# Kept partial sums added by VectorE, two small operations of a step on GpSimd, and a rearranged end, in a two-layer graph network kernel

## The reference, cut to what matters

```python
def _ggc(x, adj, W, wih, whh, bih, bhh):
    m = adj @ (x @ W)
    gi = m @ wih.T + bih
    gh = x @ whh.T + bhh
    r = sigmoid(i_r + h_r)
    z = sigmoid(i_z + h_z)
    n = tanh(i_n + r * h_n)
    return (1.0 - z) * n + z * x
h = relu(_ggc(x, adj, W1, ...)); g = relu(_ggc(h, adj, W2, ...))
x1 = layernorm(x + g)
support = x1 @ weight
mask = (adj != 0)
rank = cumsum(mask, axis=1)
deg = rank[:, -1:]
k = minimum(deg, 100)
pos = rank - (deg - k)
w = mask * where(pos > 0, 0.5 ** (k - pos), 0.0)
out = layernorm(x1 + w @ support + bias)
```

## Time and profile before

| | |
|---|---|
| median of 3 runs | 347.71 us (347.25 to 347.92) |
| profiled execution | 348.46 us, span 346.7 us |
| TensorE busy | 329.2 us, 95% of the span |
| VectorE busy | 302.2 us, 87% |
| ScalarE busy | 185.4 us, 53% |
| GpSimd busy | 27.5 us, 8% |
| DMA | 107.86 MB, mean 311 GB/s |
| granted TensorE clock | full, but for the last slice |

### The profile page before, as it was taken

The page is one execution under the profiler, slowest core; times in us unless marked ns, Lnnn a source line. Parts: engine busy times, 40 slices in busy tenths (PEclk is TensorE's granted clock), DMA queues, the critical chain, the costliest instruction groups (busy, mean ns, idle before and its releaser), DMA issues.

```text
span 346.7 us, 6773 instructions
## 1 busy us (share of the span) xinstructions
PE 329.2 (95%) x2540; PEld 154.3 (45%) x2540; DVE 302.2 (87%) x505; ACT 185.4 (53%) x243; POOL 27.5 (8%) x35
## 2 busy tenths in 40 slices
PE   1998999999999999999999999999999999999992
PEld 0442334333333333333333333545444444789992
DVE  0689879898999999997999678879989999978995
ACT  0203304105122057069458347888797969769983
POOL 2000000000000000000000001000210202013264
PEclk9999999999999999999999999999999999999997
DMA  7999999999999999999998999998999996000002
GB/s 244 414 411 408 409 408 400 384 411 393 372 372 375 366 396 358 328 346 353 317 321 288 384 401 391 353 340 325 366 373 349 364 366 215 11 7 4 2 32 93
DMA packets 32001, 107.86 MB, mean 311 GB/s; under 512 B 3553, under 2 KB 6369, under 8 KB 31969
## 3 DMA queue, kind: packets, MB, share of 16 engines
q1 hardware_dynamic: 31104, 106.15, 81.4%
q10 hardware_dynamic: 864, 1.28, 1.0%
HBM read 106.37 MB, written 1.05 MB: 310 GB/s over the span
## 4 chain that ended last, share of the span: by engine, by line
PE 70%; DMA 10%; ACT 8%; DVE 7%; issue 3%; POOLq 0%; POOL 0%; ACTq 0%; DVEq 0%; SPq 0%
PE m_acc L494 35%; PE out L494 15%; DMA stream<-in_adj_t 9%; PE out L626 6%; PE m_acc L626 4%; PE gate_ps L570 4%; PE gate_ps L577 2%; ACT wexp L806 2%; ACT codes L806 2%; DMA w<-in_w 2%; DVE run L1034 1%; PE gate_ps L599 1%; DVE codes L1179 1%; PE gate_ps L594 1%; ACT mx L766 1%
## 5 line engine op out<-in xcount | busy, mean ns | idle before, releaser
L494 PE MATMUL m_acc<-stream,s_in 128*64 128x512 f32 x488 | 119.2, 596 | 1.3 <-DMA stream<-in_adj_t 1.0
L990 DVE TENSOR_SCALAR codes<-stream 128x1024 uint8<-128x1024 f32 x109 | 72.0, 686 | 6.3 <-DMA stream<-in_adj_t 6.0
L494 PE MATMUL out<-stream,s_mid 128*64 128x512 f32 x264 | 66.3, 593 | 0.0
L494 PEld LDWEIGHTS m_acc<-stream,s_in 128*64 128x64 f32 x488 | 32.9, 137 | 63.6 <-issue 49.2
L494 PE MATMUL m_acc<-stream,s_mid 128*64 128x512 f32 x224 | 51.6, 599 | 0.0
L925 POOL TENSOR_TENSOR rstd<-stat,mhalf 128x4 f32<-128x4 f32 x16 | 24.6, 1535 | 311.7 <-DVE stat L1145 311.7
L1039 DVE SCALAR_TENSOR_TENSOR codes<-codes,run 128x384 uint32<-128x384 uint32 (+2 forms) x62 | 43.9, 709 | 2.1
L1034 DVE TENSOR_TENSOR run<-run,codes 128x768 uint16<-128x768 uint16 (+2 forms) x61 | 42.3, 694 | 2.0
L709 ACT ACTIVATE m_high<-m_acc 64x512 f32<-64x512 f32 x13 | 7.7, 594 | 56.1 <-PE m_acc L494 47.2
L494 PEld LDWEIGHTS out<-stream,s_mid 128*64 128x64 f32 x264 | 18.9, 137 | 37.0 <-issue 36.3
L743 ACT ACTIVATE rz<-gate_ps,b_rz 128x256 f32<-128x256 f32 x32 | 13.4, 468 | 36.8 <-PE gate_ps L577 36.8
(11 more groups left out here) (171 smaller groups left out, 402.3 us busy)
## 6 DMA issues: line engine op xcount, KB each, us to landing
stream<-in_adj_t SPq DMA_DIRECT2D x192, 512.0 KB, 6.1
wexp<-in_adj_t SPq DMA_DIRECT2D x2, 512.0 KB, 5.6
late<-in_adj_t SPq DMA_DIRECT2D x2, 512.0 KB, 6.5
third<-in_x_pairs SPq DMA_DIRECT2D x8, 128.0 KB, 6.3
out_nodes<-stream SPq DMA_DIRECT2D x8, 128.0 KB, 2.0
hx<-in_x_pairs ACTq DMA_DIRECT2D x1, 512.0 KB, 7.5
third<-in_adj_t SPq DMA_DIRECT2D x1, 512.0 KB, 7.8
run<-in_adj_t SPq DMA_DIRECT2D x1, 512.0 KB, 9.7
```

Of the source, the lines that this page charges most:

```text
L494: last = nc.tensor.matmul(to[D * u:D * (u + 1), :], state[:, t * D:(t + 1) * D], data[:, u * CW:(u + 1) * CW], start=start[u], stop=stop)
L990: nc.vector.tensor_scalar(edges(p // 2, b, 2 * (p % 2), 2), loaded(n), 0.0, None, ALU.not_equal).then_inc(mask_made, 1)
```

## The change

Chunks 11 to 15 (`WITH_KEPT`): ScalarE's `high` and TensorE's identity products are gone. VectorE's new `high_kept` adds the upper half of the accumulator and the kept sum into `m_high`, behind the first group of chain tiles of the step, and `combine` follows it. In steps 1 to 7 GpSimd does `split_low` and `add_bias`, in this order, behind its power. Step 1 has its chain tiles cut otherwise and ScalarE's expansions all behind its square; step 3 has one expansion more ahead of `split_high` and one fewer behind it. Which engine expands which of the later blocks is dealt anew (21 by VectorE instead of 22). The weights of block (4, 1) lie in `hx` instead of `kept`. In the end other chunks are scaled by ScalarE, and the last chunk's blocks 5 to 7 run in two halves of its nodes, each with its own bank, adds, square, sum, power, scaling and store.

```diff
+WITH_KEPT = range(NCH + 3, 2 * NCH)
+BY_POOL = 7
+PLACE[4, 1] = "h"
 BY_DVE = [AHEAD[4], AHEAD[6], AHEAD[7], AHEAD[8]] + \
-    [REST[n] for n in (2, 5, 7, 9, 11, 12, 14, 16, 18, 19, 21, 22, 24, 26, 28, 30, 32, 34)]
+    [REST[n] for n in (2, 5, 7, 9, 11)] + \
+    [(6, 5), (7, 3), (7, 4), (7, 5), (0, 6), (3, 6), (5, 6), (6, 6), (7, 6), (1, 7), (2, 7), (5, 7)]
-ACT_EXPANDS = {1: (1, 1, 1), 2: (1, 2, 2), 3: (1, 2, 3), 4: (1, 2, 2), 5: (1, 2, 2),
+ACT_EXPANDS = {1: (0, 2, 1), 2: (1, 2, 2), 3: (1, 3, 2), 4: (1, 2, 2), 5: (1, 2, 2),
-ACT_END = (1, 1, 1, 1, 1, 0, 0, 0)
-DVE_END = (2, 2, 1, 1, 1, 1, 0, 0)
+ACT_END = (1, 1, 2, 1, 1, 0, 0, 0)
+DVE_END = (1, 1, 3, 1, 1, 0, 0)
+DVE_SCALES = {5: (0,), 6: (1, 2)}
-OUT_ACT = (0, 2, 4)
+OUT_ACT = (3, 4, 5)
+LAST = NCH - 1
+SPLIT_FROM = 5
+HALVES = (slice(0, KT // 2), slice(KT // 2, KT))
-CHAIN_CUT = [(1, 2), (2, 4), (2, 3), (2, 3)] + [(1, 2)] * 3 + [(0, 1)] * 2
+CHAIN_CUT = [(1, 2), (1, 3), (2, 3), (2, 3)] + [(1, 2)] * 3 + [(0, 1)] * 2
...
-                if first and ch in KEPT:
-                    half, _, part = kept_part(ch)
-                    pe.wait_ge(m2_kept, len(KEPT))
-                    for u in range(2):
-                        nodes = slice(u * HW, (u + 1) * HW)
-                        nc.tensor.matmul(acc_bank(g)[u * D:(u + 1) * D, nodes], ident2[half, :],
-                                         part[:, nodes], start=False, stop=False)
...
+            def share_last():
+
+                for part, tiles in enumerate(HALVES):
+                    for j in range(SPLIT_FROM, NCH):
+                        if part == 0:
+                            if (j, LAST) in BY_DVE:
+                                pe.wait_ge(by_dve, BY_DVE.index((j, LAST)) + 1)
+                            else:
+                                pe.wait_ge(by_act, BY_ACT.index((j, LAST)) + 1)
+                        last = share_tiles(j, LAST, range(tiles.start, tiles.stop))
+                    last.then_inc(last_done, 1)
...
                 if t < NCH:
-                    high(g + 1)
+                    if g + 1 not in WITH_KEPT:
+                        high(g + 1)
                     state(g + 1)
...
+            def add_bias(s):
+                pool.wait_ge(x1_made, s + 1)
+                pool.wait_ge(bias_centred, 3)
...
+                nc.gpsimd.tensor_tensor(x1b_nodes(s), x1, bias_b[:, :, :], ALU.add)\
+                    .then_inc(x1b_made, 1)
+
+            def split_low(s):
+                pool.wait_ge(sup_high, s + 1)
+                nc.gpsimd.tensor_tensor(support(s)[:, :, 1, :], sup_f, support(s)[:, :, 0, :],
+                                        ALU.subtract).then_inc(sup_made, 1)
 
             for s in range(NCH):
                 to_rstd(s, 0)
+                if s < BY_POOL:
+                    split_low(s)
+                    add_bias(s)
...
+            def high_kept(g):
+                _, _, part = kept_part(2 * NCH - 1 - g)
+                dve.wait_ge(pair_used, USED[g])
+                dve.wait_ge(m2_kept, len(KEPT))
+                dve.wait_ge(m_ready, g)
+                nc.vector.tensor_tensor(m_high[0:D, :], acc_bank(g)[D:P, :], part, ALU.add)\
+                    .then_inc(high_copied, 1)
...
-                if t < NCH:
+                first, second = CHAIN_CUT[t]
+                if t < NCH and g + 1 not in WITH_KEPT:
                     combine(g + 1)
-                first, second = CHAIN_CUT[t]
                 for j, k in CHAIN[t][:first]:
                     chain(j, k)
+                if g + 1 in WITH_KEPT:
+                    high_kept(g + 1)
+                    combine(g + 1)
                 expand_next(DVE_EXPANDS[t][0])
...
                 make_x1s(t - 1)
-                add_bias(t - 1)
-                split_low(t - 1)
+                if t > BY_POOL:
+                    add_bias(t - 1)
+                    split_low(t - 1)
...
+            for i in range(LAST):
+                dve.wait_ge(block_done, AT[NCH - 1, i] + 1)
+                add_high(i)
+                if i >= 1:
+                    sum_squares(NCH + i - 1, i - 1, ysq[:, i - 1])
+                add_low(i, i)
+                expand_next(DVE_END[i])
+                for b in DVE_SCALES.get(i, ()):
+                    scale_out(b, b)
+            dve.wait_ge(last_done, 1)
+            add_high(LAST, HALVES[0])
+            add_low(LAST, LAST, HALVES[0])
+            sum_squares(NCH + LAST - 1, LAST - 1, ysq[:, LAST - 1])
+            sum_squares(NCH + LAST, LAST, ysq[:, LAST, HALVES[0]], HALVES[0])
+            dve.wait_ge(last_done, 2)
+            add_high(LAST, HALVES[1])
+            add_low(LAST + 1, LAST, HALVES[1])
+            scale_out(LAST - 1, LAST - 1)
+            sum_squares(NCH + LAST + 1, LAST, ysq[:, LAST, HALVES[1]], HALVES[1])
+            scale_out(LAST, LAST, HALVES[0])
+            scale_out(LAST + 1, LAST, HALVES[1])
```

More of the change, by code:

```diff
@@ L298, in build, with end_bank @@
         end_ps = out_ps + [m_acc[0], m_acc[1], n_ps, rz_ps]
+        def end_bank(i, t):
+            return end_ps[0] if i == LAST and t >= KT // 2 else end_ps[i]
         def m2_bank(b):
@@ L470, in _ @@
                     sp.wait_ge(o_by_dve, i + 1 - sum(a < i for a in OUT_ACT))
-                sp.dma_start(out[NCH - 1 - i], o_n[:, i]).then_inc(out_stored, 16)
-            sp.wait_ge(out_stored, 16 * NCH)
+                if i < LAST:
+                    sp.dma_start(out[NCH - 1 - i], o_n[:, i]).then_inc(out_stored, 16)
+            for part, nodes in enumerate(HALVES):
+                sp.wait_ge(o_by_dve, LAST + 1 - len(OUT_ACT) + part)
+                sp.dma_start(out[NCH - 1 - LAST, :, nodes], o_n[:, LAST, nodes])\
+                    .then_inc(out_stored, 16)
+            sp.wait_ge(out_stored, 16 * (NCH + 1))
         @blk.tensor
@@ L622, in share, with share_tiles @@
                         pe.wait_ge(x1_made, NCH)
+                        pe.wait_ge(y_made, 1)
+                share_tiles(j, i, range(KT)).then_inc(block_done, 1)
+            def share_tiles(j, i, tiles):
+                first, last_j = j == 0, j == NCH - 1
                 w, half = weights(j, i), support(j)
-                for t in range(KT):
+                per_bank = KT // 2 if i == LAST else KT
+                for t in tiles:
                     for k in range(KT):
-                        last = nc.tensor.matmul(end_ps[i][:, t * P:(t + 1) * P],
+                        last = nc.tensor.matmul(end_bank(i, t)[:, t * P:(t + 1) * P],
                                                 w[:, k * CW + t * P:k * CW + (t + 1) * P],
-                                                half[:, k, :, :], start=first and t + k == 0,
-                                                stop=last_j and t + k == 2 * KT - 2)
-                last.then_inc(block_done, 1)
+                                                half[:, k, :, :],
+                                                start=first and t % per_bank == 0 and k == 0,
+                                                stop=last_j and (t + 1) % per_bank == 0
+                                                and k == KT - 1)
+                return last
+            def share_last():
[8 more added lines that the diff above has]
+                    last.then_inc(last_done, 1)
             def pass1(b):
@@ L695, in _ @@
                 chunk2(t, FIRST[t])
-            for n in range(RING, len(ORDER)):
+            for n in range(RING, len(ORDER) - (NCH - SPLIT_FROM)):
                 if ORDER[n] in GATES_END:
@@ L701, in _ @@
                 share(*ORDER[n])
+            share_last()
         @blk.scalar
@@ new lines, in scale_out, with end_part @@
+            def scale_out(n, i, nodes=slice(0, KT)):
+                dve.wait_ge(rstd_made, NCH + n + 1)
+                nc.vector.tensor_tensor(o_n[:, i, nodes], y[:, i, nodes],
+                                        rstd[:, i, nodes].unsqueeze(2)
+                                        .to_broadcast([P, nodes.stop - nodes.start, D]),
+                                        ALU.mult).then_inc(o_by_dve, 1)
+            def end_part(i, part, nodes):
+                return halves(end_bank(i, nodes.start))[:, nodes, part, :]
```

68 lines of the change are left out of this document (35 added, 33 removed).

## The result

The changed kernel takes 349.09 us (median of six runs, 348.52 to 350.16) against 347.72 for the kernel before in the same comparison: a ratio of 1.0041, 95% interval 1.0024 to 1.0058. It is slower by 1.4 us, where 345.9, 1.8 us faster, was forecast. That 349.09 lies inside the stated range of 344.5 to 349.6 is owed to the first rival, for whose sake the range reached so high; the forecast itself went the wrong way.

A forecast was written before the change was run, and what follows sets the result against it. TensorE was taken as the bound, VectorE just keeping up; TensorE's shifts (products and waits gone, +0.5 low half, +1.8 in step 3) summed to -1.8: 347.71 to 345.9 us, stated range 344.5 to 349.6.

The forecast's parts named there:

- the first rival: Chain tiles behind make_x1s, steps 3 to 6: GpSimd holds VectorE 0.5 us for each of eight operations; 349.5 us, chance 0.30.
- What bounds the kernel: Second pass: TensorE, busy 88.85 of 90 us, is the bound; VectorE, busy 82.26, just keeps up.
- the sum has no such delay: VectorE's chain operations beside GpSimd's new ones: no delay counted, from a price between 0 and 0.43 us an operation.
- the row at 243.83: Trace row: a chain operation ran as always within GpSimd's power from 242.74 to 244.66; ground for counting no delay.
- the kept sum (0.89 for 0.7): VectorE, chunks 11 to 15: high_kept taken at 0.7 us each, 3.5 us in all, after the row of combine.
- 2.0 us early: VectorE's start of step 7 would be 2.0 us early, TensorE 1.6; stated within the first rival.
- the forecast of 345.9: Whole kernel, waits and tail as summed: 345.9 us, own range 345.0 to 346.9, chance 0.42.
- The wait of 1.8 us before chunk 13: Step 3: TensorE waits 1.8 us for VectorE's late combine(11), whose PSUM bank chunk 13 writes; counted as +1.8.
- The wait of 0.5 us in step 1: Step 1: TensorE's share waits 0.5 us (bounds 0 and 1.4) for GpSimd's low half; counted as +0.5.
- my 1.1: GpSimd's new operations, such as the low half: 1.1 us taken, between bounds of 0.31 and 1.92.
- the tail is hardly shorter: Behind TensorE's end: 3.7 us for 3.9 before, so the kernel's end is at -1.8.
- its 16.7 us from the first to the last `add_high`: The end: 17.6 us before, 16.7 after, with VectorE's expansions 7 for 8 (-1.14) and one scaling more (+0.33).

The follow-up runs named there:

- e5: Changed kernel with kept sum and combine ahead of the step's first chain tiles, one expansion each of steps 4 and 5 moved from VectorE to ScalarE; 347.26 us.
- e7: Changed kernel with identity products and ScalarE's copy back, GpSimd's two operations kept, two expansions (steps 4, 5) moved from VectorE to ScalarE; 346.20 us.
- e8: Changed kernel with GpSimd's bias sum and low half replaced by memsets of the same outputs, which read nothing; 345.42 us.
- e10: Changed kernel with GpSimd's bias sum done twice in each step, the second waiting for the first; 350.67 us.
- e4: Changed kernel with the kept sum and combine ahead of the step's first chain tiles; 349.62 us.
- e3: Changed kernel with kept sums and GpSimd's operations both undone, leaving the new deal of expansions, step 1's order and the end in halves; 346.08 us, ratio 0.9949.
- e1: Changed kernel with GpSimd's two operations (bias sum, low half) back on VectorE, kept sums staying on VectorE; 351.44 us.

## Why the prediction was wrong, point by point

**What bounds the kernel** was read too much for TensorE. The slack of nothing at `node` was seen and stated, but it was used only as a warning. The kernel has two engines that are both full there: before the change TensorE was busy for 88.85 us of the 90, and VectorE, with 82.26, started `n_input` of steps 5 to 7 (268.30, 284.41 and 298.94) straight behind its own work, without a wait for anyone. The change took 0.58 us a chunk from one and gave 0.89 to the other. e5 and e7 show that VectorE's length is the bound with the kept sums and not without.

**The term that failed** is the sentence "the sum has no such delay": of the bounds 0 and 0.43 us an operation I took 0, by the row at 243.83, where a 4-element power left VectorE alone. The price is 0.35 us for each of the two operations in steps 3 to 5 (1.22 to 1.58) and 0.5 for each in step 6. The row was the wrong nearest one: the operation at 243.83 ran on for 0.39 us behind the power's end at 244.66, and above all the power reads 4 elements of a partition, the new operations 256. A step of VectorE was to become 0.1 us shorter and became 0.67 longer (16.11 to 16.78 or 16.79): 0.70 by collisions, 0.19 by the kept sum (0.89 for 0.7), less 0.11 by which the offload saved more than 0.79 (0.90). So `n_input` of step 7, counted from step 1, was not 2.0 us early but 0.9 late (92.12 against 91.20), and TensorE stood at `node`.

**The first rival was what happened**: its place (the chain tiles behind `make_x1s` in steps 3 to 5; in step 6 it was the expansions) and its order of size (0.5 us assumed, 0.35 and 0.5 found). That its result came so close (349.5 for 349.09) is in part luck: the eight operations cost 3.1 us and not 4.0, the kept sums 0.19 more each than the sum had, and the part from step 8 on was about 1 us better, and these errors offset one another. e8 and e10, which take GpSimd's reads away and add one, move the time by -3.7 and +1.6. With the reads gone, e8's 345.42 stands close to the forecast of 345.9, which had left out just this cost; some 0.5 us of that is the shorter wait for the memset. The rival had got 0.30 against 0.42.

**The Trainium skill**, SBUF — State Buffer, section Who interferes with whom, had spoken for that rival, and should have been given more weight than a row of another size. What the runs show is milder than its sentence that the loser is blocked for the whole of the other instruction: the bias sum lasts 0.72 us where nothing stands beside it (308.43 in the changed kernel), and VectorE lost 0.35 by it. The rows of step 3 above suggest how the two go together: the bias sum started at 246.08 beside a chain operation that ended at 247.20, and ended itself 0.59 us later, at 247.79; the 0.35 us are lost by the chain operation that started between, at 247.30. Each engine seems to wait for the other in turn, GpSimd for a long instruction and VectorE for what is left of a short one. No run tests that reading by itself. Its remark that an instruction of GpSimd that only writes does not collide with such a reading fits e8.

**The wait of 1.8 us before chunk 13** was right as an event (2.00) and wrong as a term of a sum: e4 takes it away and the time stays. A wait adds to the time only where nothing behind it waits for the same engine again.

**The wait of 0.5 us in step 1** came out at 0.54; the low half took 0.87 us for my 1.1, beside short chain operations that it held up. **The end**: "the tail is hardly shorter" said 3.7 us, it is 3.35, and from step 8 on the rearrangement brings about 1.1 us (38.3 to 37.2) where my sum had next to nothing (its 16.7 us from the first to the last `add_high` should have been 16.8: 17.6 less 1.14, plus 0.33). The powers did run one behind another (2.55 us for three), as said. This end, step 1's order and the dealing of the expansions are the good part of the change: 0.5% by e3.

**A rest that stays open**: steps 1 to 8 and the rest together make the changed kernel 0.7 us slower, the medians 1.4. The stretch before step 1, with the same code, is 0.7 us shorter in the profiled execution after than in that of before, which makes the two spans equal; it explains nothing of the medians' difference. The other 0.7 us are not found. One thing that differs between executions is the granted clock. In the profiled executions of e1, e5 and e10 it fell to the lower level for some 3 us, four times in all, each time shortly behind a wait of TensorE of 1.9 to 2.1 us (289.52, 300.87, 241.26 and 288.54). Other waits as long or longer (241.24 in the changed kernel, 243.54 in e1) had no such fall behind them, and no run shows what the falls add to the medians of the kernels that wait.

## What to carry to other kernels

Where two engines are both above 90% busy in a stretch, as TensorE (99%) and VectorE (91%) were here, a saving on one is worth nothing until the other's length of step is written down beside it; take the length from the same operation of one step to that of the next, in the trace. Work moved to GpSimd is not free to VectorE even if nobody waits for it: price each such operation by its reading beside VectorE's two-operand and expanding instructions, and by a row that reads as much. The largest wait in the list need not be the one that costs; shifting it away (e4) is the cheapest test.

## What the runs showed that was not expected

A GpSimd operation with two operands of 128x256 elements made a VectorE chain operation 0.35 us longer (1.22 to 1.57), whether the VectorE operation was of 16 or 32 bit elements. It made an expansion, which has a single 8 bit operand, 0.5 us longer (a pair with two such operations beside it: 2.35 to 3.37). GpSimd itself was held up more than VectorE: the bias sum went from 0.72 alone to 1.71, and to 2.77 beside the long operation of step 2; the low half from 0.87, beside short chain operations, to 1.13. A GpSimd operation that only writes is not always free of this. In e8 two memsets ran unhindered beside a chain operation, but this one, in step 7, took 0.88 us for 0.31, beside an expansion of VectorE:

```profile
303.24 1.22 DVE L1248 TENSOR_SCALAR stream<-codes 128x2048 uint16<-128x2048 uint8 x1
...
303.82 0.88 POOL L980 MEMSET s_mid<- 128x256 f16 x1 [1.23 <-ACT s_mid L827]
```

The Trainium skill's GPSIMD Engine Reference, section Performance versus the Vector engine, gives a sum of two tensors of 2048 float32 elements as about two times slower on GpSimd than on VectorE. At the 256 elements of this case the bias sum took 0.72 us alone and VectorE 0.43, 1.7 times as long.
